# A transformer block on one core: a steady tile's scores wait for the values alone, and the orders of four engines are written anew

## The chip, the cores and the metric

The kernel runs on one core of a Trainium2 chip. The metric is the device time of one execution in microseconds (us), the median of three runs.

## What is computed

For 128 sequences of 64 tokens with 256 channels, everything in float32:

```python
n1 = g1(cond) * x / rms(x) + b1(cond)
x1 = x + softmax(q k^T / 4) v @ Wo.T              # 16 heads of 16
n2 = g2(cond) * x1 / rms(x1) + b2(cond)
out = x + x1 + (silu(n2 @ gate.T) * (n2 @ hid.T)) @ out.T   # hidden width 1024
```

g1, b1, g2 and b2 are small linear maps of a 64-wide condition of each sequence.

## The kernel before

**Tiles.** 16 tiles of 8 sequences (512 tokens). Products are made of float32 values split in a high part and a low rest (three passes: high by high, high by low, low by high), so most matrices exist as `_hi` and `_lo`. In PSUM eight banks are shared out by hand.

**Pipeline.** Tile t does its attention while the MLP of tile u = t - 1 runs between its pieces. Five instruction streams are written by hand: TensorE (PE), ScalarE (ACT), VectorE (DVE), GpSimd (POOL), SyncE (SP, all transfers). Each stream has functions for single pieces and four lists that call them: `first_tile` (t = 0, attention alone), `steady_tile` (t = 1 to 14; 2 to 14 in a loop), `last_tile` (t = 15) and `after_last` (the MLP of tile 15). Each engine works its list strictly in order, and each piece begins with semaphore waits. What decides the time is therefore which piece stands behind which on the same engine.

**Pieces on PE.** `gate(u, j)` and `hid(u, j)` are six matmuls of 512 columns each (lines 1221 to 1240), for chunk j of the hidden width. `down(u, j)` is twelve of 256 columns (lines 1082 to 1084). `scores(t, r)` (line 1183) is 64 small ones for half r of the heads, `transpose_probs(t, p)` (line 1193) four transposes, `values_probs(t, r)` (line 1208) 64 small ones. `project_q`, `project_k` (lines 1110 to 1113, six matmuls of 512 columns) and `project_v` (twelve of 256 columns) make the next tile's queries, keys and values, `project_out` (24 of 256 columns) closes this tile's attention, and `transpose_norm2(t, c)` (line 1102) turns the normed rows.

**Gate path.** gate(u, j), then tanh (ACT, line 506), silu (DVE, line 836), hidden (DVE, line 843, which needs hid too), high_hidden (ACT, line 511), low_hidden (POOL, line 284), then down(u, j). gate(u, j + 1) waits for silu(u, j), since the gate has one bank; hid(u, j + 1) waits for hidden(u, j).

**Softmax path.** scores, row_maxima and shift (DVE, lines 806, 813), exp (ACT, line 516), reciprocals (DVE, lines 820, 825), divide (POOL, line 290), transpose_probs, keep_transposed (ACT, line 521), values_probs, high_attention (ACT, line 526), low_attention (DVE, line 830), project_out.

**Norm paths.** Next tile: squares1 (ACT), next_inverse (POOL), two transfers that spread the factors, scale_rows (DVE, line 737), first_norm1 (DVE, lines 756 and 763) and second_norm1 (ACT, line 451), high_norm1 (ACT), low_norm1 (POOL), projections. This tile, behind project_out: first_residual (DVE, line 894), squares2 (ACT, line 442), inverse2 (POOL, lines 264, 267), scale_second (ACT, line 553) with scale_second_rest (DVE, line 746), transpose_norm2, second_norm2 (ACT, line 451) and first_norm2 (DVE), high_norm2 (ACT, line 477), low_norm2 (POOL line 278, DVE line 777). The last piece of ACT's list is `first_values(t + 1)` (line 500), which copies half the next tile's values from PSUM; DVE's is `second_values` (line 800).

**Start of a tile.** `scores(t, 0)` is PE's first piece. In a steady tile it waits for seven counts, one after the other:

```python
pe.wait_ge(k_act_done, t + 1)
pe.wait_ge(k_dve_done, t + 1)
pe.wait_ge(q_act_done, t + 1)
pe.wait_ge(q_dve_done, t + 1)
pe.wait_ge(v_act_done, t + 1)
pe.wait_ge(v_dve_done, t + 1)
pe.wait_ge(x1_done, 2 * t)
```

**SP.** In its order, each with its wait: the transposed input of the next tile, the store of a finished tile (waits for results), the next input x (waits for keep_input and squares1), then the factors out and back in (waits for next_inverse). In the first tile the output weights' transfer stands ahead of these.

Of the kernel before, what the change touches and what calls it, by code (L numbers as in the profile page):

```python
# [53 lines left out]
def conditioned_block(nc, x, xT, condT, modT, attW, gateT, hidT, outT, consts, out):  # L54
# [3 lines left out]
    with ExitStack() as ctx:  # L58
# [196 lines left out]
        def _(pool):  # L255
# [92 lines left out]
            def steady_tile(t, finish, ahead):  # L348
                u = t - 1
                sum_of_inputs(u)  # L350
                low_hidden(u, 0)
                divide(t, 0)
                divide(t, 1)
                low_hidden(u, 1)
                divide(t, 2)
                next_inverse(t)
                divide(t, 3)
                low_hidden(u, 2)
                low_hidden(u, 3)
                divide(t, 4)  # L360
                low_hidden(u, 4)
# [5 lines left out]
                low_hidden(u, 5)  # L367
                low_hidden(u, 6)
                inverse2(t)
# [3 lines left out]
            def last_tile(t, finish, ahead):  # L373
                u = t - 1
                divide(t, 0)
                low_hidden(u, 0)
                divide(t, 1)
                divide(t, 2)
                low_hidden(u, 1)
                divide(t, 3)  # L380
                low_hidden(u, 2)
                sum_of_inputs(u)
                divide(t, 4)
                low_hidden(u, 3)
                divide(t, 5)
                low_hidden(u, 4)
                divide(t, 6)
                divide(t, 7)
                low_hidden(u, 5)
# [32 lines left out]
        def _(act):  # L422
# [139 lines left out]
            def first_tile(t, ahead):  # L562
                u = t - 1
                high_hid_weights()
                keep_input(t)
                first_values(0)
                exp(t, 0)
                exp(t, 1)
                squares1(t + 1)
                exp(t, 2)  # L570
                exp(t, 3)
                exp(t, 4)
                keep_transposed(t, 0)
                keep_transposed(t, 1)
                high_out_weights()
                exp(t, 5)
                exp(t, 6)
                keep_transposed(t, 2)
                keep_transposed(t, 3)
                high_attention(t, 0)  # L580
                exp(t, 7)
                keep_transposed(t, 4)
                keep_transposed(t, 5)
                second_norm1(t + 1)
                high_norm1(t + 1, 0)
                high_norm1(t + 1, 1)
                keep_transposed(t, 6)
                keep_transposed(t, 7)
                high_attention(t, 1)
# [9 lines left out]
            def steady_tile(t, finish, ahead):  # L599
# [3 lines left out]
                high_hidden(u, 0)  # L603
# [3 lines left out]
                exp(t, 2)  # L607
                high_hidden(u, 1)
                tanh(u, 2)
                exp(t, 3)  # L610
                squares1(t + 1)
                tanh(u, 3)
                keep_transposed(t, 0)
                keep_transposed(t, 1)
                high_hidden(u, 2)
                tanh(u, 4)
                keep_transposed(t, 2)
                keep_transposed(t, 3)
                high_hidden(u, 3)
                high_attention(t, 0)  # L620
                exp(t, 4)
                exp(t, 5)
                tanh(u, 5)
                high_hidden(u, 4)
# [4 lines left out]
                exp(t, 6)  # L629
                exp(t, 7)  # L630
                high_hidden(u, 5)
                tanh(u, 6)
# [3 lines left out]
                high_hidden(u, 6)  # L636
                tanh(u, 7)
                first_queries(t + 1)
                high_attention(t, 1)
                first_keys(t + 1)  # L640
                squares2(t)
                scale_second(t)
                high_hidden(u, 7)
# [5 lines left out]
            def last_tile(t, finish, ahead):  # L649
# [3 lines left out]
                tanh(u, 1)  # L653
                high_hidden(u, 0)
                exp(t, 1)
                exp(t, 2)
                tanh(u, 2)
                high_hidden(u, 1)
# [823 lines left out]
```

## Time and profile before

| | us |
|---|---|
| median of three runs | 959.45 (959.16 to 959.62) |
| the profiled execution's own time | 959.58 |
| its span (first to last profiled instruction) | 957.5 |
| PE busy in the span | 908.0 |
| DVE, ACT, POOL busy | 664.8, 559.4, 451.9 |
| tile 1 to tile 15, start of scores to start of scores | 79.64 to 870.88 |
| last instruction of PE | 953.18 |

How to read it: the first 80 us are weights and tile 0, then 14 steady tiles repeat, then come tile 15 and the MLP that is left. An engine's busy time is the union of its instructions; a matmul's end is modelled and overlaps the start of the next by 0.16 us here, so the spacing of starts is the better measure. Times named as "at 41.8" below are counted from the start of scores(t, 0) of a tile.

### The profile page before, as it was taken

What the parts mean: (1) busy time and instruction counts of PE and PEld (TensorE: products, weight loads), DVE (VectorE), ACT (ScalarE), POOL (GpSimd) and SP (SyncE); (2) the same over time, 40 slices, a digit from 0 to 9 for tenths busy, and PEclk for the clock granted to TensorE, in tenths of its full rate; (3) what the DMA queues carried; (4) which work ended last, traced back from release to release, by engine and by line L of the source; (5) the groups of instructions that cost most, each with busy time, mean ns of one, the idle gap of its engine ahead of it and who ended that gap; (6) DMA issues with size and microseconds to landing.
All of it is one profiled execution on the core that took longest, in us unless ns stands there. A gap on an engine that the chain in (4) does not pass through costs nothing.

```text
span 957.5 us, 24194 instructions
## 1 busy us (share of the span) xinstructions
PE 908.0 (95%) x8988; PEld 773.5 (81%) x8988; DVE 664.8 (69%) x1082; ACT 559.4 (58%) x1255; POOL 451.9 (47%) x394
## 2 busy tenths in 40 slices
PE   5678999999999999999999999999999999999998
PEld 4466888878888887888888888888888888788887
DVE  3647768576875857778586877858687685868652
ACT  4556656656665666656566655655666566565542
POOL 4454525354463545436354543535455354544433
PEclk9779999999999999999999999999999999999999
DMA  5300101010110101011010111101010010200000
GB/s 191 98 26 23 34 25 56 1 55 22 44 33 22 39 16 55 22 44 33 7 47 22 44 32 44 33 0 55 22 44 33 23 53 0 55 0 1 24 23 23
DMA packets 25595, 34.06 MB, mean 36 GB/s; under 512 B 3296, under 2 KB 20896, under 8 KB 25440
## 3 DMA queue, kind: packets, MB, share of 16 engines
q1 hardware_dynamic: 25344, 33.59, 11.2%
q8 instruction: 18, 0.29, 0.1%
q10 hardware_dynamic: 224, 0.10, 0.0%
q14 instruction: 9, 0.07, 0.0%
HBM read 25.27 MB, written 8.42 MB: 35 GB/s over the span
## 4 chain that ended last, share of the span: by engine, by line
PE 82%; ACT 6%; issue 5%; DVE 3%; POOL 2%; DMA 1%; ACTq 1%; DVEq 0%; SPq 0%; POOLq 0%
PE ps L1082 8%; PE ps L1084 7%; PE ps L1083 7%; PE ps L1221 7%; PE ps L1237 6%; PE ps L1193 6%; PE ps L1227 6%; PE ps L1222 6%; PE ps L1240 6%; PE ps L1238 6%; PE ps L1183 4%; PE ps L1110 4%; PE ps L1208 4%; PE ps L1111 3%; PE ps L1113 3%
## 5 line engine op out<-in xcount | busy, mean ns | idle before, releaser
L284 POOL TENSOR_TENSOR h_lo<-h,h_hi 128x512 fp32r<-128x512 f32 x128 | 165.7, 1295 | 142.4 <-ACT h_hi L511 142.4
L290 POOL TENSOR_TENSOR probs<-probs,recip 128x512 f32<-128x512 f32 x128 | 134.5, 1058 | 105.6 <-DVE recip L825 105.5
L1082 PE MATMUL ps<-out_w_hi,h_hi 128*128 128x256 f32 x512 | 147.2, 287 | 0.7
L1084 PE MATMUL ps<-out_w_hi,h_lo 128*128 128x256 f32 x512 | 144.4, 282 | 0.0
L1083 PE MATMUL ps<-out_w_lo,h_hi 128*128 128x256 f32 x512 | 144.1, 281 | 0.0
L506 ACT ACTIVATE shared<-ps 128x512 f32<-128x512 f32 x128 | 76.1, 595 | 99.7 <-PE ps L1227 99.4
L836 DVE SCALAR_TENSOR_TENSOR shared<-shared,ps 128x512 f32<-128x512 f32 x128 | 87.4, 683 | 46.4 <-ACT shared L506 44.9
L516 ACT ACTIVATE probs<-probs 128x512 f32<-128x512 f32 x128 | 80.7, 631 | 62.5 <-DVE probs L813 61.9
L1221 PE MATMUL ps<-xn_hi,gate_w_hi 128*128 128x512 f32 x256 | 110.2, 430 | 0.4 <-DVE shared L836 0.2
L843 DVE SCALAR_TENSOR_TENSOR h<-shared,ps 128x512 f32<-128x512 f32 x128 | 87.4, 683 | 30.1 <-PE ps L1240 28.7
L1237 PE MATMUL ps<-xn_hi,hid_w_hi 128*128 128x512 f32 x256 | 105.1, 410 | 0.0
L1082 PEld LDWEIGHTS ps<-out_w_hi,h_hi 128*128 128x128 f32 x512 | 96.5, 188 | 8.2 <-POOL h_lo L284 6.5
L1222 PE MATMUL ps<-xn_hi,gate_w_lo 128*128 128x512 f32 x256 | 101.1, 395 | 0.0
L1238 PE MATMUL ps<-xn_hi,hid_w_lo 128*128 128x512 f32 x256 | 100.5, 393 | 0.0
L1083 PEld LDWEIGHTS ps<-out_w_lo,h_hi 128*128 128x128 f32 x512 | 96.4, 188 | 1.5
L1084 PEld LDWEIGHTS ps<-out_w_hi,h_lo 128*128 128x128 f32 x512 | 96.4, 188 | 0.0
L806 DVE TENSOR_REDUCE row_max<-ps 128x8 f32<-128x512 f32 x128 | 83.7, 683 | 17.5 <-PE ps L1183 17.2
L511 ACT CAST h_hi<-h 128x512 fp32r<-128x512 f32 x128 | 79.5, 622 | 25.6 <-DVE h L843 25.1
L820 DVE TENSOR_REDUCE sums<-probs 128x8 f32<-128x512 f32 x128 | 86.3, 674 | 3.4 <-ACT probs L516 1.9
L813 DVE TENSOR_TENSOR probs<-ps,row_max 128x512 f32<-128x512 f32 x128 | 87.3, 684 | 1.6 <-PE ps L1193 1.6
L1193 PE MATMUL ps<-consts_sb,probs 128*128 128x128 f32 x512 | 74.2, 282 | 8.2 <-POOL probs L290 8.1
L521 ACT COPY probsT<-ps 128x512 f32<-128x512 f32 x128 | 70.9, 587 | 17.4 <-PE ps L1193 17.4
(92 smaller groups left out, 2016.6 us busy)
## 6 DMA issues: line engine op xcount, KB each, us to landing
x_in<-in_x SPq DMA_DIRECT2D x16, 512.0 KB, 3.4
xT_in<-in_xT SPq DMA_DIRECT2D x16, 512.0 KB, 3.2
out<-result SPq DMA_DIRECT2D x15, 512.0 KB, 3.0
inv_all<-inv_rows SPq DMA_DIRECT2D x15, 256.0 KB, 3.8
shared<-in_attT SPq DMA_DIRECT2D x1, 1024.0 KB, 7.8
shared<-in_gateT SPq DMA_DIRECT2D x1, 1024.0 KB, 9.7
shared<-in_hidT SPq DMA_DIRECT2D x1, 1024.0 KB, 5.0
shared<-in_outT SPq DMA_DIRECT2D x1, 1024.0 KB, 5.7
```

Of the source, the lines that this page charges most:

```text
L284: nc.gpsimd.tensor_tensor(h_lo[:, j % KEPT, :], h[:, j % 2, :], h_hi[:, j % KEPT, :].bitcast(F32), ALU.subtract).then_inc(h_lo_done, 1)
L290: nc.gpsimd.tensor_tensor(own, own, recip[:, p % TOGETHER, :].unsqueeze(2).to_broadcast([P, SEQS, L]), ALU.mult).then_inc(divided, 1)
L836: nc.vector.scalar_tensor_tensor(act_g[:, :], act_g[:, :], 1.0, ps[:, GATE, :], ALU.add, ALU.mult).then_inc(silu_done, 1)
L843: nc.vector.scalar_tensor_tensor(h[:, j % 2, :], act_g[:, :], 0.5, ps[:, HIDDEN, :], ALU.mult, ALU.mult).then_inc(h_done, 1)
L1082: nc.tensor.matmul(dst, a_hi, b_hi, start=first, stop=False, skip_group_check=skip)
L1083: nc.tensor.matmul(dst, a_hi, b_lo, start=False, stop=False, skip_group_check=skip)
L1084: return nc.tensor.matmul(dst, a_lo, b_hi, start=False, stop=last, skip_group_check=skip)
L1193: last = nc.tensor.transpose(ps[:, bank_of(t, p), k * P:(k + 1) * P], probs[:, p % TOGETHER, k * P:(k + 1) * P], ident)
L1221: nc.tensor.matmul(ps[:, GATE, :], gate_w_hi[:, i, w], xn2_hi[:, i, :], start=i == 0, stop=False)
L1222: nc.tensor.matmul(ps[:, GATE, :], gate_w_lo[:, i, w], xn2_hi[:, i, :], start=False, stop=False)
L1237: nc.tensor.matmul(ps[:, HIDDEN, :], hid_w_hi[:, i, w], xn2_hi[:, i, :], start=i == 0, stop=False)
L1238: nc.tensor.matmul(ps[:, HIDDEN, :], hid_w_lo[:, i, w], xn2_hi[:, i, :], start=False, stop=False)
```

## The change

Two things. The first steady-tile wait is cut from seven counts to two:

```diff
                 elif r == 0:
-                    pe.wait_ge(k_act_done, t + 1)
-                    pe.wait_ge(k_dve_done, t + 1)
-                    pe.wait_ge(q_act_done, t + 1)
-                    pe.wait_ge(q_dve_done, t + 1)
+                    pe.wait_ge(v_dve_done, t + 1)
                     pe.wait_ge(v_act_done, t + 1)
-                    pe.wait_ge(v_dve_done, t + 1)
-                    pe.wait_ge(x1_done, 2 * t)
```

The lists of PE, ACT, DVE and POOL are written anew in all four functions; SP's is not touched, and every piece is called as often as before. Of `steady_tile`, in the order of the calls (T is transpose_probs, VP values_probs, KT keep_transposed, rm row_maxima, sh shift, rc reciprocals, low_h low_hidden):

```
PE before: scores0 gate0 hid0 gate1 hid1 down0 gate2 hid2 T0 gate3 T1 hid3 gate4 T2 T3 hid4
           scores1 VP0 gate5 down1 down2 hid5 down3 gate6 T4 T5 down4 hid6 q0 T6 T7 gate7 VP1
           q1 k0 project_out down5 hid7 k1 v1 tnorm0 tnorm1 v0 down6 down7
PE after:  scores0 gate0 hid0 gate1 hid1 T0 gate2 hid2 down0 gate3 hid3 T1 T2 gate4 T3 hid4
           scores1 VP0 down1 down2 gate5 down3 down4 hid5 T4 T5 gate6 hid6 q0 k0 T6 T7 gate7
           VP1 q1 hid7 project_out k1 v1 down5 tnorm0 tnorm1 v0 down6 down7

ACT before: tanh0 exp0 high0 keep_input tanh1 exp1 exp2 high1 tanh2 exp3 squares1 tanh3 KT0 KT1
            high2 tanh4 KT2 KT3 high3 high_attention0 exp4 exp5 tanh5 high4 second_norm1
            high_norm1(0,1) KT4 exp6 exp7 high5 tanh6 KT5 KT6 KT7 high6 tanh7 first_queries
            high_attention1 first_keys squares2 scale_second high7 second_norm2 high_norm2(0,1)
            first_values
ACT after:  tanh0 exp0 keep_input tanh1 exp1 high0 high1 tanh2 exp2 squares1 KT0 exp3 high2 tanh3
            KT1 tanh4 KT2 KT3 high_attention0 high3 exp4 exp5 high4 tanh5 second_norm1
            high_norm1(0,1) KT4 exp6 tanh6 exp7 KT5 KT6 KT7 first_keys tanh7 high_attention1
            high5 first_queries squares2 scale_second high6 high7 second_norm2 high_norm2(0,1)
            first_values

DVE before: low_norm2 results rm0 rm1 sh0 silu0 hidden0 rm2 rm3 rc0 sh1 silu1 sh2 hidden1 rc1 sh3
            silu2 rc2 hidden2 rc3 silu3 hidden3 silu4 hidden4 rm4 rm5 sh4 rm6 rc4
            low_attention0 sh5 scale_rows rc5 silu5 first_norm1 sh6 rm7 hidden5 sh7 rc6 rc7
            silu6 hidden6 low_attention1 second_queries first_residual silu7
            scale_second_rest hidden7 second_keys first_norm2 second_values
DVE after:  low_norm2 results rm0 rm1 sh0 silu0 hidden0 rc0 sh1 silu1 rm2 hidden1 sh2 rm3 rc1
            silu2 hidden2 sh3 rc2 rc3 silu3 hidden3 silu4 hidden4 rm4 rm5 sh4 sh5 scale_rows
            rc4 rc5 low_attention0 first_norm1 silu5 rm6 hidden5 sh6 rm7 sh7 rc6 rc7 silu6
            hidden6 low_attention1 silu7 second_queries first_residual hidden7 second_keys
            scale_second_rest first_norm2 second_values

POOL before: sum_of_inputs low_h0 divide0 divide1 low_h1 divide2 next_inverse divide3 low_h2
             low_h3 divide4 low_h4 divide5 low_norm1(0,1) divide6 divide7 low_h5 low_h6
             inverse2 low_h7 low_norm2
POOL after:  sum_of_inputs divide0 low_h0 low_h1 divide1 next_inverse divide2 divide3 low_h2
             low_h3 low_h4 divide4 divide5 low_norm1(0,1) divide6 divide7 low_h5 inverse2
             low_h6 low_h7 low_norm2
```

Of `first_tile`, what the prediction speaks of:

```diff
 ACT:
+                exp(t, 0)
                 high_hid_weights()
                 keep_input(t)
+                exp(t, 1)
+                exp(t, 2)
+                squares1(t + 1)
                 first_values(0)
-                exp(t, 0)
-                exp(t, 1)
-                squares1(t + 1)
-                exp(t, 2)
                 exp(t, 3)
...
 POOL:
-                low_hid_weights()
                 divide(t, 0)
                 divide(t, 1)
+                divide(t, 2)
                 next_inverse(t)
-                divide(t, 2)
                 divide(t, 3)
+                low_hid_weights()
                 divide(t, 4)
...
 PE:
                 scores(t, 0)
+                project_v(0, 1)
                 project_q(0, 1)
-                project_v(0, 1)
+                transpose_probs(t, 0)
                 project_v(0, 0)
                 scores(t, 1)
-                transpose_probs(t, 0)
                 transpose_probs(t, 1)
...
                 project_v(t + 1, 1)
+                project_v(t + 1, 0)
                 transpose_norm2(t, 0)
                 transpose_norm2(t, 1)
-                project_v(t + 1, 0)
```

`last_tile` is reordered along the same lines (transposes later among the gates, project_out followed by hid7, down3 and down4, then transpose_norm2; results(t - 2) moves to the front of DVE's list). In `after_last` four `down` pieces move by one place and results(t - 2) moves ahead of silu(u, 1).

## Rows read from the trace of the kernel before

**Rows 1.** Busy time by stretch: a steady tile, then tile 15 (stretch, length, engines, clock).
```profile
250.00:306.45 56.45, 55.52 (x561) 47.43 (x561) 41.19 (x67) 34.42 (x78) 26.99 (x24) 1.00 0.10 33
...
870.88:918.54 47.66, 46.70 (x513) 39.98 (x513) 33.02 (x59) 25.63 (x55) 22.86 (x20) 1.00 0.04 13
```

**Rows 2.** Timeline (start, length, instruction) at the end of the tile from 250.00.
```profile
300.28 1.04 PE L1102 MATMUL ps<-consts_sb,shared 128*128 128x128 f32 x8
...
304.92 1.19 ACT L500 COPY values<-ps 64x512 f32<-64x512 f32 x2
...
306.45 1.20 PE L1183 MATMUL ps<-keys,queries 32*64 32x128 f32 x64 [0.86 <-ACT values L500]
```

**Rows 3.** Timeline, the start of that tile: first instructions of PE's pieces, and silu(u, 0).
```profile
252.62 0.40 PE L1237 MATMUL ps<-xn_hi,hid_w_hi 128*128 128x512 f32 x1
...
254.19 0.50 PE L1221 MATMUL ps<-xn_hi,gate_w_hi 128*128 128x512 f32 x1
...
255.68 0.40 PE L1237 MATMUL ps<-xn_hi,hid_w_hi 128*128 128x512 f32 x1
...
257.31 0.39 PE L1082 MATMUL ps<-out_w_hi,h_hi 128*128 128x256 f32 x1
...
258.83 0.39 PE L1221 MATMUL ps<-xn_hi,gate_w_hi 128*128 128x512 f32 x1
...
260.23 0.39 PE L1237 MATMUL ps<-xn_hi,hid_w_hi 128*128 128x512 f32 x1
...
253.45 0.69 DVE L836 SCALAR_TENSOR_TENSOR shared<-shared,ps 128x512 f32<-128x512 f32 x1 [0.23 <-ACT shared L506]
```

**Rows 4.** Timeline of PE, the middle: T4 and T5, down4, hid6, q0, T6 and T7, gate7.
```profile
279.89 1.03 PE L1193 MATMUL ps<-consts_sb,probs 128*128 128x128 f32 x8
280.68 0.37 PE L1082 MATMUL ps<-out_w_hi,h_hi 128*128 128x256 f32 x1
...
282.31 0.50 PE L1237 MATMUL ps<-xn_hi,hid_w_hi 128*128 128x512 f32 x1
...
283.87 0.50 PE L1110 MATMUL ps<-xn_hi,att_w_hi 128*128 128x512 f32 x1
...
285.37 1.16 PE L1193 MATMUL ps<-consts_sb,probs 128*128 128x128 f32 x8
286.29 0.48 PE L1221 MATMUL ps<-xn_hi,gate_w_hi 128*128 128x512 f32 x1
```

**Rows 5.** Timeline: first matmuls of project_out and of down5 behind it, and scale_second.
```profile
291.78 0.28 PE L1082 MATMUL ps<-att_w_hi,attT_hi 128*128 128x256 f32 x1
...
294.62 0.28 PE L1082 MATMUL ps<-out_w_hi,h_hi 128*128 128x256 f32 x1
...
297.92 0.91 ACT L553 ACTIVATE shared<-shared,inv 128x256 f32<-128x256 f32 x2 [1.46 <-POOL inv L267]
```

**Rows 6.** Timeline behind scores(t, 1): rm4 and rm5, high_attention0; and the sums of rc6.
```profile
270.29 1.29 DVE L806 TENSOR_REDUCE row_max<-ps 128x8 f32<-128x512 f32 x2 [0.39 <-PE ps L1183]
...
271.35 0.59 ACT L526 CAST attT_hi<-ps 128x512 fp32r<-128x512 f32 x1 [2.38 <-PE ps L1208]
...
282.77 0.68 DVE L820 TENSOR_REDUCE sums<-probs 128x8 f32<-128x512 f32 x1
```

**Rows 7.** Timeline of DVE and POOL: scale_rows and divide7 of tile 0, divide5 and first_norm1.
```profile
53.02 1.97 DVE L737 TENSOR_TENSOR xn<-xT_in,inv_all 128x1024 f32<-128x1024 f32 x1
53.18 2.72 POOL L290 TENSOR_TENSOR probs<-probs,recip 128x512 f32<-128x512 f32 x1 [1.88 <-DVE recip L825]
...
278.03 1.04 POOL L290 TENSOR_TENSOR probs<-probs,recip 128x512 f32<-128x512 f32 x1
...
278.25 1.37 DVE L756 TENSOR_TENSOR xn<-xn,mod 128x512 f32<-128x512 f32 x1
279.76 0.69 DVE L763 TENSOR_TENSOR xn<-xn,mod 128x512 f32<-128x512 f32 x1
```

**Rows 8.** Timeline of tile 0: low_hid_weights, squares1, scores(0, 1).
```profile
28.13 4.60 POOL L297 TENSOR_TENSOR hid_w_lo<-shared,hid_w_hi 128x2048 fp32r<-128x2048 f32 x1 [2.40 <-ACT hid_w_hi L433]
...
35.46 0.42 ACT L442 ACTIVATE squares<-x_in 128x256 f32<-128x256 f32 x1 [0.45 <-DMA x_in<-in_x]
35.52 1.97 PE L1183 MATMUL ps<-keys,queries 32*64 32x128 f32 x64 [2.89 <-DVE queries L791]
```

More of the change, by code:

```diff
@@ L367, in steady_tile @@
                 low_hidden(u, 5)
+                inverse2(t)
                 low_hidden(u, 6)
-                inverse2(t)
                 low_hidden(u, 7)
@@ L606, in steady_tile @@
                 exp(t, 1)
-                exp(t, 2)
+                high_hidden(u, 0)
                 high_hidden(u, 1)
                 tanh(u, 2)
+                exp(t, 2)
+                squares1(t + 1)
+                keep_transposed(t, 0)
                 exp(t, 3)
-                squares1(t + 1)
+                high_hidden(u, 2)
                 tanh(u, 3)
-                keep_transposed(t, 0)
                 keep_transposed(t, 1)
-                high_hidden(u, 2)
                 tanh(u, 4)
@@ L679, in last_tile @@
                 tanh(u, 6)
-                keep_input(t)
                 high_attention(t, 1)
-                high_hidden(u, 5)
+                tanh(u, 7)
                 high_hidden(u, 6)
                 squares2(t)
-                tanh(u, 7)
                 scale_second(t)
@@ L966, in steady_tile @@
                 shift(t, 4)
[L967 to L969 removed]
                 shift(t, 5)
                 scale_rows(t + 1)
+                reciprocals(t, 4)
                 reciprocals(t, 5)
+                low_attention(t, 0)
+                first_norm1(t + 1)
                 silu(u, 5)
[L974 removed]
+                row_maxima(t, 6)
+                hidden(u, 5)
                 shift(t, 6)
                 row_maxima(t, 7)
[L977 removed]
                 shift(t, 7)
@@ L995, in last_tile @@
                 low_norm2(u)
+                results(t - 2)
                 row_maxima(t, 0)
@@ L998, in last_tile @@
                 shift(t, 0)
+                silu(u, 0)
                 shift(t, 1)
-                silu(u, 0)
-                row_maxima(t, 2)
                 hidden(u, 0)
                 reciprocals(t, 0)
+                silu(u, 1)
+                reciprocals(t, 1)
+                hidden(u, 1)
+                row_maxima(t, 2)
                 row_maxima(t, 3)
-                silu(u, 1)
+                silu(u, 2)
                 shift(t, 2)
-                hidden(u, 1)
-                reciprocals(t, 1)
+                hidden(u, 2)
+                shift(t, 3)
                 reciprocals(t, 2)
-                silu(u, 2)
-                shift(t, 3)
-                hidden(u, 2)
+                silu(u, 3)
                 reciprocals(t, 3)
-                silu(u, 3)
-                results(t - 2)
                 hidden(u, 3)
                 silu(u, 4)
+                hidden(u, 4)
                 row_maxima(t, 4)
@@ L1020, in last_tile @@
                 shift(t, 4)
+                shift(t, 5)
+                low_attention(t, 0)
                 row_maxima(t, 6)
-                hidden(u, 4)
-                shift(t, 5)
                 reciprocals(t, 4)
-                reciprocals(t, 5)
                 row_maxima(t, 7)
@@ L1036, in last_tile @@
                 hidden(u, 6)
+                silu(u, 7)
                 first_residual(t)
-                silu(u, 7)
                 hidden(u, 7)
@@ L1396, in last_tile @@
                 values_probs(t, 1)
+                gate(u, 7)
+                project_out(t, ahead)
+                hid(u, 7)
                 down(u, 3)
-                project_out(t, ahead)
-                gate(u, 7)
-                hid(u, 7)
                 down(u, 4)
```

164 lines of the change are left out of this document (80 added, 84 removed).

## Prediction

> **What bounds the kernel now.** I read the engines' busy times first: TensorE is busy 55.5 of 56.45 us in a steady tile, at full granted clock, and no other engine over 42 [rows 1]. The fourteen steady tiles repeat this to 0.02 us (the first is 1 us longer), so one of them, from 250.00, is read piece by piece. TensorE's own work is left as it is; what a new order can give is its idle time, which is seen in the spacing of starts, not in the modelled ends. An undisturbed gate or hid piece takes 1.40 us (258.83 to 260.23) [rows 3]. Three places are longer.
>
> 1. The end: scores(t, 0) starts with 0.86 us of idle time before it, released by first_values on ScalarE [rows 2]; the same line recurs at the start of 15 tiles. The values end at 304.92 + 1.19 = 306.11 and the scores start at 306.45, so 0.34 us pass between a release and its use. Between silu(u, 0), which ends at 254.14, and gate(u, 1), at 254.19, only 0.05 us pass [rows 3].
> 2. The start: hid(u, 0) takes 1.57 (waiting for silu) and gate(u, 1) 1.49, since a piece that follows a stall loses a further 0.1. hid(u, 1) takes 1.63 because down0 waits for the low part on GpSimd, and down0 then 1.52 against 1.42 [rows 3].
> 3. The middle: down4 takes 1.63 where 1.42 and 0.09 for coming behind transposes are due, hid6 1.56, q0 1.50, and T6 with T7 0.92 where T4 with T5 take 0.79 [rows 4]: 0.12 + 0.16 + 0.10 + 0.13 = 0.51 us.
>
> **The change in a steady tile, step by step.** Times "at" count from the start of scores(t, 0).
>
> Start. gate1 still waits for silu0 (the path gate, tanh, silu is not shortened): 0.26 us stay. down0 moves behind hid2, three pieces later, and T0 comes into its place. divide0 is now first behind the input sum on GpSimd and would be ready at 7.0, T0 is wanted at 7.1. So (1.63 - 1.40) + (1.52 - 1.42) = 0.33 goes. Gain 0.33.
>
> Middle. down1 to down4 and hid5 come ahead of T4, and q0 with k0 ahead of T6, so low parts, divides and low_norm1 all get 1 to 2 us more. The 0.51 us go, if the other engines are not later than now. Gain 0.51.
>
> What could make them later is scale_rows, now directly behind sh5. In the trace divide7 of tile 0 starts 0.16 us after a scale_rows and takes 2.72 instead of 1.04 us, to 0.9 us after its end; and first_norm1's first half, started 0.22 us after a divide, takes 1.37 instead of 0.69 [rows 7]. So of two such instructions the later one is held. In the new order: row maxima 4 and 5 and two shifts stand ahead of scale_rows, each 0.60 us after the other [rows 6], so it comes 2.40 us after rm4. high_attention0 starts 1.06 us after rm4 (271.35 - 270.29), then come its 0.5, high3's 0.6 and a handover of 0.1: low_h3 starts 2.25 us after rm4, first by 0.15 us. So scale_rows is held: 1.3 - 0.15 - 0.15 = about 1.0 us. Later first_norm1 meets divide5 as it does now, 0.7 us. Without holding silu5 would end 2.4 + 2.0 + 2 x 0.9 (two reciprocals [rows 6]) + 0.6 + 1.25 + 0.7 = 8.7 us after rm4; gate6 is wanted at 0.9 + 0.1 + 2.84 + 1.40 + 2.84 + 1.40 + 0.79 = 10.3 after rm4. The slack is 1.55 and the holds are 1.65 to 1.7: loss 0.1 us. (If VectorE came first, low_h3 would be held to 4.4 + 1.2 = 5.6 after rm4 where down3 wants it at 5.3: loss 0.3 and 0.1 for the stall, so 0.3 more than I take.)
>
> The Trainium skill has this as a rule ("SBUF — State Buffer", section "Who interferes with whom"): a VectorE instruction with two SBUF inputs and a GpSimd instruction that reads SBUF exclude each other, and whoever issues first blocks the other fully. It speaks against packing scale_rows beside low_h3 and low_h4. The trace agrees: 2.72 against 1.04 us [rows 7].
>
> Tail. project_out starts at 41.78 now (291.78 - 250.00) [rows 5]. New: 41.78 - 0.33 - 0.51 + 1.40 (hid7 now ahead of it) + 0.10 = 42.44. Behind it now come down5, hid7, k1, v1, and transpose_norm2 starts 8.50 after project_out (300.28 - 291.78) [rows 2, 5], though scale_second was ready at 7.05 (298.83 - 291.78). New: project_out 2.84 (294.62 - 291.78), k1 1.40, v1 1.42, down5 1.42: 7.08, a dead heat with the 7.05 + 0.05 of the chain residual, squares2, inverse2, scale_second. I take 7.10. From transpose_norm2 to the end of first_values it is 5.83 us (306.11 - 300.28) [rows 2], the same ScalarE pieces as before; high6 and high7 fit in the gap ahead of second_norm2. TensorE itself needs 0.8 + 1.5 + 1.4 + 1.5 = 5.2, so ScalarE still sets the start of the next tile.
>
> The wait. The removed counts are met long before; what they cost is that two more waits stand behind v_act_done. With v_act_done last, the handover should shrink from 0.34 towards the 0.05 of silu to gate [rows 2, 3]. Bounds: 0 (the start of 64 small matmuls is what costs) and 0.29. I take 0.29, since the handover with one wait is the nearest row.
>
> Period: 42.44 + 7.10 + 5.83 + 0.05 = 55.42 against 56.45, so 1.03 us a tile, and 14 tiles give 14.4 us.
>
> **Tile 0.** exp0 now precedes the hid weights' cast and keep_input on ScalarE, so SP's transfer of x is issued near 33.8 (29.0 now), and squares1, which waits for that transfer now already [rows 8], stands ahead of first_values: about 3.4 us of landing and 1.7 of squares put scores(0, 1) near 40 instead of 35.5. Against that, T0 runs early, and shift4, which waits for T0, is 1.3 us late instead of 4.5. low_hid_weights (4.60 us on GpSimd [rows 8]) goes from an idle stretch to a place before divide4, and divides 6 and 7 then meet scale_rows, each held in turn. Before transpose_norm2 v0 now stands, where TensorE sat idle. Bounds 0 (all absorbed by TensorE's idle stretches) and +4.6 (scores' delay in full); taken +1.6.
>
> **Tile 15 and after.** Tile 15 spans 47.66 with TensorE busy 46.70 [rows 1]; results ahead of the maxima lets silu0 come in time (0.2), down0 is put behind, and transpose_norm2 meets its chain. Bounds 0 and -1.5, taken -1.0. In after_last the stalls gate, tanh, silu, gate stay three in number: 0.
>
> **Sum.** 959.58 (the profiled execution, 2.1 above its span and 0.13 above the median) - 14.4 + 1.6 - 1.0 = 945.8. Median and profiled execution agree so well that no shift is made.
>
> **Rivals.** A difference of 0.2% (1.9 us) is about what a measurement of this kernel can tell from none.
> - A, forecast: 945.8, between 941 (no holds, tile 0 free) and 950. For it: stall by stall the trace shows what goes. Chance 0.52.
> - B, the handover stays 0.34: 14 x 0.29 = 4.1 more, 949.9. For it: the scores have a load of weights per small matmul. Against it: silu to gate. 0.12.
> - C, VectorE is first in the pair, or T0 or transpose_norm2 loses its dead heat each time: 0.3 a tile more, 950. 0.12.
> - D, only the wait counts; the new order loses in the middle what it gains: 14 x 0.29 = 4.1 and tile 0's loss: 959.6 - 4.1 + 1.6 - 1.0 = 956.1. 0.10.
> - E, slower: one more hold. If add_shift or scale_rows meets a second GpSimd piece (low_h4 follows low_h3 by one exp and one cast), 1.1 us falls straight on gate6, since the slack of 1.55 is spent. The period is then 56.5, and 14 x 0.07 + 0.6 = 1.6 us are lost: 961.2. It decides from holds of 2.6 us a tile (1.55 of slack and 1.03 of gain) on. Against it: the reciprocals lie between the pairs. 0.08. (By the rule of the Trainium skill above, the one that issues later is blocked fully, so such a further hold would cost its whole length.)
> - F, gains and losses of D and E mix to nothing: 0.03. G, better than 941 because DVE's list has slack I counted as spent: 0.03.
>
> **How the numbers follow.** Faster: A, B, C, D, G = 0.89; same 0.03, with a piece of D and E 0.04; slower 0.07. The range 941 to 956 leaves out E, F, G and part of D.
>
> **What would show it.** In the changed profile: starts of scores 55.4 us apart; the idle time before scores 0.6 to 0.7, first_values to scores 0.05; down0 at 1.42 and no stall around T6; scale_rows 2.9 us long beside low_h3; project_out at 42.4 and transpose_norm2 7.1 behind it; scores(0, 1) near 40. Wrong would be: scale_rows at 2.0 (then the period is 55.3), an idle line before gate6 of over 0.3, or scores 0.3 us behind first_values still.

## The result and the profile after

| | before | after |
|---|---|---|
| median of the comparison's 4 runs, us | 959.54 (959.16 to 961.56) | 949.56 (947.61 to 950.45) |
| ratio to before | | 0.9886 [0.9867, 0.9905] |
| span of the profiled execution | 957.5 | 947.4 |

The change makes the kernel 10.0 us faster; 13.7 were forecast. The range held the time, and the direction and most of the mechanism were right. TensorE still makes up most of the chain that ended last (87%, 82% before); GpSimd's busy time has grown from 451.9 to 488.0 us, though it does the same work. From the page of the kernel after (engines, costliest groups):

```profile
PE 900.7 (95%) x8988; PEld 772.5 (82%) x8988; DVE 675.1 (71%) x1082; ACT 552.1 (58%) x1255; POOL 488.0 (52%) x394
...
L284 POOL TENSOR_TENSOR h_lo<-h,h_hi 128x512 fp32r<-128x512 f32 x128 | 192.0, 1505 | 206.4 <-ACT h_hi L511 204.9
```

Where the 10 us come from is read in windows from one start of scores(t, 0) to the next, which is what [rows 1] show of the kernel before. Columns: length, then busy time (count) of PE, PE's loads, DVE, ACT and POOL, then granted clock, DMA share, GB/s. Tile 0, tile 1, tile 4 and tile 15 of the kernel after:

```profile
26.70:81.88 55.18, 34.00 (x400) 28.11 (x399) 33.74 (x54) 29.73 (x66) 25.98 (x18) 0.70 0.16 53
81.88:139.23 57.35, 56.82 (x560) 48.92 (x561) 40.73 (x66) 33.71 (x78) 29.54 (x24) 0.96 0.08 25
250.27:305.81 55.54, 54.84 (x560) 47.28 (x561) 41.82 (x68) 33.93 (x78) 29.50 (x24) 1.00 0.11 33
861.13:908.40 47.27, 46.60 (x512) 39.93 (x513) 33.61 (x60) 25.63 (x55) 23.01 (x20) 1.00 0.04 13
```

In the kernel before tile 0 (from 26.96) took 52.68, tile 1 57.45. So, by spans:

| stretch | before | after | difference | forecast |
|---|---|---|---|---|
| up to the first scores | 26.96 | 26.70 | -0.26 | 0 |
| tile 0 | 52.68 | 55.18 | +2.50 | +1.6 |
| tile 1 | 57.45 | 57.35 | -0.10 | -1.03 |
| tiles 2 to 14, each | 56.44 | 55.53 | -0.91, 13 times: -11.9 | -1.03, 13 times: -13.4 |
| tile 15 | 47.66 | 47.27 | -0.39 | -1.0 |
| MLP of tile 15, end | 38.96 | 39.00 | +0.04 | 0 |

These spans fall short of the forecast by 3.7 us, which lie in four places: 0.9 in tile 0, 0.9 in tile 1, 1.5 in the loop, 0.6 in tile 15 (against them, 0.3 ahead of the first scores, a stretch that takes 25.75 to 27.45 in the profiles of this study although no edit touches it).

**The end of a steady tile.** The timeline of the kernel after from 348 to 362 (start, length, engine, line, operation; in brackets the idle time before it and what ended it). This tile starts at 305.81, so project_out stands at 42.40 and transpose_norm2 7.10 behind it:

```profile
348.21 0.28 PE L1082 MATMUL ps<-att_w_hi,attT_hi 128*128 128x256 f32 x1
...
354.34 0.91 ACT L553 ACTIVATE shared<-shared,inv 128x256 f32<-128x256 f32 x2 [1.46 <-POOL inv L267]
...
355.31 1.09 PE L1102 MATMUL ps<-consts_sb,shared 128*128 128x128 f32 x8
...
360.00 1.19 ACT L500 COPY values<-ps 64x512 f32<-64x512 f32 x2
...
361.33 0.93 PE L1180 MATMUL ps<-keys,queries 32*64 32x128 f32 x45 [0.66 <-ACT values L500]
```

The values end at 360.00 + 1.19 = 361.19 and the scores start at 361.33: the handover, 0.34 in [rows 2], is 0.14 now, not the 0.05 that was forecast. transpose_norm2 has no idle line and yet starts 0.06 behind the end of scale_second (355.25): the dead heat that was forecast.

**The middle.** The other engines in the same tile, where the forecast had two holds (one of two instructions waits for the other inside its own run), and then the first matmul of project_k(t + 1, 0):

```profile
328.07 1.30 POOL L284 TENSOR_TENSOR h_lo<-h,h_hi 128x512 fp32r<-128x512 f32 x1 [5.66 <-ACT h_hi L511]
328.23 2.99 DVE L737 TENSOR_TENSOR xn<-xT_in,inv_all 128x1024 f32<-128x1024 f32 x1
...
329.63 2.76 POOL L284 TENSOR_TENSOR h_lo<-h,h_hi 128x512 fp32r<-128x512 f32 x1 [0.26 <-ACT h_hi L511]
...
332.35 2.56 POOL L290 TENSOR_TENSOR probs<-probs,recip 128x512 f32<-128x512 f32 x2
...
333.33 0.68 DVE L756 TENSOR_TENSOR xn<-xn,mod 128x512 f32<-128x512 f32 x1
...
334.15 1.31 DVE L763 TENSOR_TENSOR xn<-xn,mod 128x512 f32<-128x512 f32 x1
...
335.38 0.67 DVE L836 SCALAR_TENSOR_TENSOR shared<-shared,ps 128x512 f32<-128x512 f32 x1
...
339.75 0.57 ACT L521 COPY probsT<-ps 128x512 f32<-128x512 f32 x1
...
340.46 0.47 PE L1110 MATMUL ps<-xn_hi,att_w_hi 128*128 128x512 f32 x1
```

low_hidden(u, 3) starts first, by 0.16 us, and scale_rows takes 2.99 instead of 1.97. Then the hold is handed on: low_hidden(u, 4), started while scale_rows is still running, takes 2.76 for 1.29. first_norm1 is held in its second half (1.31 for 0.68) and not in its first. silu(u, 5) ends at 335.38 + 0.67 = 336.05 and gate(u, 6) runs at 336.14, directly behind T5, with no gap: with a handover of 0.05, 0.04 us of its slack are left. project_q and project_k(t + 1, 0) together take 2.94 (from 339.00 to 341.94) where two undisturbed pieces take 2.80: project_k waits for keep_transposed(t, 5), which ends at 340.32, and starts at 340.46. This stall of 0.14 was not forecast.

**Tile 0 and tile 15** of the kernel after, where the forecast took +1.6 and -1.0:

```profile
37.03 0.42 ACT L442 ACTIVATE squares<-x_in 128x256 f32<-128x256 f32 x1 [2.50 <-DMA x_in<-in_x]
...
38.64 1.16 ACT L500 COPY values<-ps 64x512 f32<-64x512 f32 x2
...
40.05 2.02 PE L1180 MATMUL ps<-keys,queries 32*64 32x128 f32 x64 [3.54 <-ACT values L500]
...
47.75 4.53 POOL L297 TENSOR_TENSOR hid_w_lo<-shared,hid_w_hi 128x2048 fp32r<-128x2048 f32 x1
...
52.24 6.27 POOL L290 TENSOR_TENSOR probs<-probs,recip 128x512 f32<-128x512 f32 x4
...
901.41 1.29 POOL L284 TENSOR_TENSOR h_lo<-h,h_hi 128x512 fp32r<-128x512 f32 x1
901.48 1.65 DVE L746 TENSOR_SCALAR shared<-shared,inv 128x256 f32<-128x256 f32 x2 [0.97 <-POOL inv L267]
...
903.22 0.96 PE L1102 MATMUL ps<-consts_sb,shared 128*128 128x128 f32 x7 [0.61 <-issue]
```

squares1 waits 2.50 us for x with first_values behind it, and scores(0, 1) start at 40.05 (35.52 in [rows 8]). low_hid_weights keeps divide(0, 4) until 52.24. In tile 15 scale_second_rest starts 0.07 us behind low_hidden(u, 6) and takes 1.65 us; transpose_norm2 follows it. The last line's "issue" names no cause: that TensorE waited for scale_second_rest is read from the order of the starts, and tried in the last experiment.

### The profile page after: what moved, and what is told of

It is laid out like the page before. It is cut to its first block, busy times and chain, and to the rows that moved or that the text cites. A ratio compares the mean times of both kernels' runs of the same rounds, so it can differ in the third digit from the quotient of the medians.

```text
span 947.4 us, 24151 instructions
## 1 busy us (share of the span) xinstructions
PE 900.7 (95%) x8988; PEld 772.5 (82%) x8988; DVE 675.1 (71%) x1082; ACT 552.1 (58%) x1255; POOL 488.0 (52%) x394
## 4 chain that ended last, share of the span: by engine, by line
PE 87%; ACT 6%; issue 2%; DVE 2%; DMA 1%; POOL 1%; ACTq 1%; SPq 0%; DVEq 0%
PE ps L1082 8%; PE ps L1084 7%; PE ps L1083 7%; PE ps L1218 7%; PE ps L1224 6%; PE ps L1234 6%; PE ps L1219 6%; PE ps L1237 6%; PE ps L1235 6%; PE ps L1190 6%; PE ps L1180 4%; PE ps L1110 4%; PE ps L1205 3%; PE ps L1111 3%; PE ps L1113 3%; ACT shared L451 3%
## 5 line engine op out<-in xcount | busy, mean ns | idle before, releaser
L284 POOL TENSOR_TENSOR h_lo<-h,h_hi 128x512 fp32r<-128x512 f32 x128 | 192.0, 1505 | 206.4 <-ACT h_hi L511 204.9
L290 POOL TENSOR_TENSOR probs<-probs,recip 128x512 f32<-128x512 f32 x128 | 141.1, 1117 | 69.2 <-DVE recip L825 68.8
L1234 PE MATMUL ps<-xn_hi,hid_w_hi 128*128 128x512 f32 x256 | 102.6, 401 | 0.0
L511 ACT CAST h_hi<-h 128x512 fp32r<-128x512 f32 x128 | 77.0, 613 | 16.2 <-DVE h L843 16.2
```

The lines of the kernel that those rows point to most:

```text
L284: nc.gpsimd.tensor_tensor(h_lo[:, j % KEPT, :], h[:, j % 2, :], h_hi[:, j % KEPT, :].bitcast(F32), ALU.subtract).then_inc(h_lo_done, 1)
L290: nc.gpsimd.tensor_tensor(own, own, recip[:, p % TOGETHER, :].unsqueeze(2).to_broadcast([P, SEQS, L]), ALU.mult).then_inc(divided, 1)
L1234: nc.tensor.matmul(ps[:, HIDDEN, :], hid_w_hi[:, i, w], xn2_hi[:, i, :], start=i == 0, stop=False)
```

## The experiments

The experiments were run in three groups, in which the kernel before took 960.86 (1 to 4), 959.76 (5 to 8) and 959.93 us (9 to 12). Differences of under 2 us between groups are therefore read from the traces and not from the medians. "Period" is the mean length of tiles 2 to 14.

**1 and 2. The wait alone, and the order alone.** The two waits in the kernel before, and the seven in the kernel after:

```diff
 # 1: before.  2: the same block, reversed, in after
                 elif r == 0:
-                    pe.wait_ge(k_act_done, t + 1)
...
-                    pe.wait_ge(x1_done, 2 * t)
+                    pe.wait_ge(v_dve_done, t + 1)
+                    pe.wait_ge(v_act_done, t + 1)
```

> The kernel before with the two counts of the change in place of the seven, all orders as before. Theory W (each wait that stands behind the last release costs about 0.1 us at the handover, and one is left): first_values to scores 0.15 us instead of 0.34, period 56.26 instead of 56.44, in all 14 to 15 x 0.19 = 2.8 us faster. Rival W0 (the handover is the start of 64 small matmuls): period 56.44, no change. Rival W1 (my prediction's figure): 0.05 us of handover, period 56.15, 4.1 us faster.

> The changed kernel with its seven counts back. Theory W: handover 0.34 again, period 55.53 + 0.19 = 55.72, 2.7 us slower than the changed kernel. Rival W0: 55.53. If the gain of the new order rested on the cut waits (another rival), the period would go up by more than 0.3.

Measured: with the wait alone 956.63 us, ratio 0.995 [0.9934, 0.9967], period 56.23; with the order alone 952.16 us, 0.991 [0.9894, 0.9927], period 55.74. A steady tile's end in the first:

```profile
249.80 1.20 ACT L500 COPY values<-ps 64x512 f32<-64x512 f32 x2
...
251.14 1.11 PE L1178 MATMUL ps<-keys,queries 32*64 32x128 f32 x59 [0.65 <-ACT values L500]
```

and in the second:

```profile
248.89 1.19 ACT L500 COPY values<-ps 64x512 f32<-64x512 f32 x2
...
250.43 1.20 PE L1183 MATMUL ps<-keys,queries 32*64 32x128 f32 x64 [0.85 <-ACT values L500]
```

251.14 - 251.00 = 0.14, and 250.43 - 250.08 = 0.35: the handover goes with the waits, whichever order stands around it. Both ways the waits are worth 0.21 us a tile (56.44 - 56.23, 55.74 - 55.53), so the two parts add up: of the 0.91 the wait brings 0.21 and the order 0.70. Rival D (only the wait counts) falls. In total, 1 is 4.2 us faster than before, which would fit rival W1's 4.1; its handover (0.14, not 0.05) and its period speak against W1, and 14 tiles by 0.21 are 2.9 us only. Where the rest came from is not shown: in the one profiled run tile 0 and tile 1 were longer than before, not shorter.

**3. The kernel after with the first tile's four lists of before.**

```diff
 def first_tile(t):      # PE, ACT, DVE, POOL
-    (the four lists of after)
+    (the four lists of before)
```

> The changed kernel with the four lists of tile 0 as before. Theory C (tile 0's new order costs 2.5 us in tile 0 itself and its longer idle stretches leave the clock low into tile 1): scores to scores 52.7 in tile 0 and 56.5 in tile 1 (57.35 with the new tile 0), 3.1 us faster than the changed kernel, about 946.5. Rival C0 (tile 1's first period is as long as it is for another reason): tile 1 stays at 57.35, 2.3 us faster.

Measured: 945.96 us (945.26 to 947.83), 0.985 [0.9834, 0.9867]. Tile 0 takes 53.70, and tile 1:

```profile
79.74:135.13 55.39, 54.84 (x561) 47.38 (x561) 40.76 (x66) 33.69 (x78) 29.64 (x24) 1.00 0.08 26
```

The median is 3.6 us below after: tile 0 is shorter by 1.5 and tile 1, whose lists are the same in both, by 2.0. The difference in tile 1 is in the third last column, the granted clock: 1.00 against 0.96. The total met the expectation (3.1), but neither part did: tile 0 was put at 52.7 and tile 1 at 56.5, and the two misses cancel.

The gain in tile 1 can't be put down to the old lists. Kernels before and 1 have these same lists in tile 0 and took 57.45 and 58.23 in tile 1, 1.0 and 2.0 us above their steady tiles. Here are the first scores of tile 1 in 1 and then in 3, after the same idle time:

```profile
80.39 2.02 PE L1178 MATMUL ps<-keys,queries 32*64 32x128 f32 x64 [3.29 <-ACT values L500]
```

```profile
79.74 1.20 PE L1180 MATMUL ps<-keys,queries 32*64 32x128 f32 x64 [3.29 <-ACT values L500]
```

So after 3.29 us without work the granted clock had fallen in one profile (0.50 in the 2 us from these scores on) and not in the other (1.00). With the new lists the idle time is 4.73 to 4.94 us, and in all eight profiles that have it (after, 2, and 4 to 9) tile 1 is 1.6 to 1.9 us longer than a steady tile. Tile 0 varies in the same way: with the old lists it took 52.68, 53.87 and 53.70 (before, 1, 3), with the new ones 55.10 to 55.18 in five profiles. So the new lists make tile 0 of the kernel after longer by 1.3 to 2.5 us, depending on the profile of the old ones that it is compared with.

**4. low_hid_weights at another place of the first tile.**

```diff
 # GpSimd, first_tile
     next_inverse(t)
-    divide(t, 3)
     low_hid_weights()
+    divide(t, 3)
     divide(t, 4)
```

> The changed kernel with low_hid_weights one place up in tile 0, between next_inverse and divide3, where GpSimd sits idle for 6.6 us. Theory L (divides 4 to 7 behind the 4.5 us of low_hid_weights collide with scale_rows): divide4 starts near 48 instead of 52.2, scale_rows and first_norm1 lose less holding, tile 0 is 0.8 us shorter. Rival L0 (tile 0's second half hangs on exp5, which waits for the fourth transpose): 0 to 0.2 us shorter.

Measured: 948.86 us, 0.9878 [0.9862, 0.9895]. divide(0, 4) comes at 47.05 instead of 52.24, yet tile 0 is only 0.44 us shorter (54.74), between theory L (0.8) and rival L0 (0 to 0.2): the second attention half then waits for keep_transposed, which stands behind second_norm1 on ScalarE. The forecast blamed this piece in part; it is a small part.

**5. A new end of the steady tile.** In the kernel after ScalarE's chain from project_out sets the next tile's start, so project_out goes one piece earlier, and down(u, 5) behind transpose_norm2, where TensorE was idle. project_out's wait for VectorE's queries is needed only from its third block on.

```diff
 # TensorE, steady_tile
     project_q(t + 1, 1)
-    hid(u, 7)
     project_out(t, ahead)
+    hid(u, 7)
     project_k(t + 1, 1)
     project_v(t + 1, 1)
-    down(u, 5)
     transpose_norm2(t, 0)
     transpose_norm2(t, 1)
+    down(u, 5)
 # project_out
-    if ahead: pe.wait_ge(q_dve_done, t + 2)
     for k in range(BLK):
+        if ahead and k == 2: pe.wait_ge(q_dve_done, t + 2)
 # VectorE: second_queries ahead of silu 7, scale_second_rest ahead of second_keys
```

> The changed kernel with a steady tile's end laid out anew: project_out waits for the queries' copy only ahead of its second half, and starts where hid7 stood; hid7, k1, v1, transpose_norm2, then down5, v0, down6, down7; DVE takes second_queries ahead of silu7 and scale_second_rest ahead of second_keys. Theory S (ScalarE's 5.9 us from transpose_norm2 on set the start of the next tile, and TensorE idles 0.6 us for it): project_out at 41.0 instead of 42.4, transpose_norm2 at 48.1 instead of 49.5, and 6.6 us of TensorE work behind it cover the chain: period 54.8 instead of 55.53, 14 x 0.73 = 10 us faster than the changed kernel, and no wait of scores for the values. Rival S0 (project_out cannot start earlier, the copies of the queries hold it): period 55.5 or above. Rival S1 (the residual chain is late for the earlier transposes): a stall before transpose_norm2 takes the place of the one before scores, period 55.2 or more.

Measured: 941.52 us (939.85 to 942.75), 0.9811 [0.979, 0.9831], 8.0 us better than after where 10 were expected; the period is 54.96 and not 54.8. A steady tile:

```profile
303.40:358.36 54.96, 54.93 (x561) 47.20 (x560) 41.35 (x67) 33.91 (x78) 29.52 (x24) 1.00 0.11 33
```

```profile
344.42 0.38 PE L1082 MATMUL ps<-att_w_hi,attT_hi 128*128 128x256 f32 x1
...
350.67 0.91 ACT L553 ACTIVATE shared<-shared,inv 128x256 f32<-128x256 f32 x2 [1.46 <-POOL inv L267]
351.63 1.09 PE L1102 MATMUL ps<-consts_sb,shared 128*128 128x128 f32 x8
```

project_out stands at 41.02 and transpose_norm2 at 48.23, 1.3 us earlier than in after (49.50). The 0.66 us of idle time before the scores are gone: TensorE is busy 54.93 of 54.96 us. So the end of the tile was bound by ScalarE's chain as argued, and a steady tile shows no idle time between its pieces any more. Short stalls inside them stay: project_out takes 2.95 us here (344.42 to 347.37) and 2.84 in after.

**6. silu(u, 5) one row maximum later** (tests the slack before gate(u, 6)).

```diff
 # VectorE, steady_tile
     first_norm1(t + 1)
-    silu(u, 5)
     row_maxima(t, 6)
+    silu(u, 5)
```

> The changed kernel with silu(u, 5) one place later, behind row_maxima(t, 6), 0.60 us. Theory M (the holds have eaten the whole slack of silu5 before gate6, as I reckoned): gate6 0.57 us later, period 56.1, 8 us slower than the changed kernel. Rival M0 (there is slack left there): period 55.53.

Measured: 955.96 us, 0.9962 [0.9948, 0.9976], 6.4 us slower than after, period 56.00, 0.47 more than after for an edit of 0.60 us. In a steady tile:

```profile
337.82 0.67 DVE L836 SCALAR_TENSOR_TENSOR shared<-shared,ps 128x512 f32<-128x512 f32 x1
...
338.54 0.51 PE L1218 MATMUL ps<-xn_hi,gate_w_hi 128*128 128x512 f32 x1 [0.32 <-DVE shared L836]
```

gate(u, 6) now waits for silu, released 0.05 us after its end, and starts at 30.89 in its tile instead of 30.33: 0.56 later, as theory M has it (0.57). The slack that the holds leave is therefore 0.04 us. The period loses less, 0.47, since project_q and project_k(t + 1, 0) take 2.79 here and not 2.94: the stall ahead of project_k in after is gone. So the slack before gate(u, 6) is spent, which was rival E's condition; rival E would have needed one more hold.

**7. scale_rows one reciprocal later** (takes it out of the way of low_hidden(u, 3)).

```diff
 # VectorE, steady_tile
     shift(t, 5)
-    scale_rows(t + 1)
     reciprocals(t, 4)
+    scale_rows(t + 1)
     reciprocals(t, 5)
```

> The changed kernel with scale_rows one place later, behind reciprocals(t, 4), so that it starts after low_h3 has ended. Theory P (a DVE instruction with two SBUF inputs is held by a GpSimd piece that started before it, here for 1.0 us): scale_rows takes 2.0 instead of 3.0 us, silu5 ends about 0.5 us earlier, and the period stays within 0.05 of 55.53 since TensorE has work until then. Rival P0 (scale_rows is long for another reason, its rows of factors): still 3.0 us, silu5 later, period 55.9 or more.

Measured: 951.90 us, 0.9915 [0.9898, 0.9932], period 55.79: slower than after by 0.26 a tile, where nearly nothing was expected.

```profile
328.94 1.30 POOL L284 TENSOR_TENSOR h_lo<-h,h_hi 128x512 fp32r<-128x512 f32 x1 [5.66 <-ACT h_hi L511]
...
330.44 2.00 DVE L737 TENSOR_TENSOR xn<-xT_in,inv_all 128x1024 f32<-128x1024 f32 x1
330.50 3.10 POOL L284 TENSOR_TENSOR h_lo<-h,h_hi 128x512 fp32r<-128x512 f32 x1 [0.25 <-ACT h_hi L511]
```

scale_rows is back at 2.00: its 2.99 was the hold. But it is now 0.06 us ahead of low_hidden(u, 4), which takes 3.10 us and ends 0.34 us later in the tile than in after, and down(u, 4) waits for it: down(u, 3) and down(u, 4) take 3.25 us together instead of 2.89. silu(u, 5) comes 0.27 later in its tile, where theory P had it 0.5 earlier, because both halves of first_norm1 are held now (1.40 and 1.31). That the hold is there is shown; the expectation's sum missed what stands behind it.

**8. first_values ahead of squares1 in the first tile** (on top of 4).

```diff
 # ScalarE, first_tile
     exp(t, 2)
-    squares1(t + 1)
     first_values(0)
+    squares1(t + 1)
```

> The kernel of the run before it in this study (low_hid_weights between next_inverse and divide3) with first_values ahead of squares1 on ScalarE in tile 0. Theory X (squares1 waits for the transfer of x, issued 4.5 us later than before, and holds first_values and with it scores(0, 1)): scores(0, 1) near 38.0 instead of 40.0, tile 0 2 us shorter than with the changed kernel. Rival X0 (tile 0 hangs on the factors' two transfers behind squares1, or on the softmax chain further on): scores(0, 1) 2 us earlier and tile 0 under 0.5 us shorter.

Measured: 946.67 us, 0.9867 [0.985, 0.9883]; tile 0 takes 52.38, 2.36 less than in 4.

```profile
36.23 1.17 ACT L500 COPY values<-ps 64x512 f32<-64x512 f32 x2 [1.47 <-PE ps L1084]
37.42 0.42 ACT L442 ACTIVATE squares<-x_in 128x256 f32<-128x256 f32 x1
37.77 1.20 PE L1180 MATMUL ps<-keys,queries 32*64 32x128 f32 x64 [1.59 <-DVE values L800]
```

Counted from scores(0, 0), scores(0, 1) start at 10.84 (13.21 in 4, 13.35 in after), and run in 1.20 us for 2.02 in after. Tile 0 is shorter by as much as they are earlier, which rules out rival X0. So the values, which did not need the transfer of x and stood behind the piece that did, held up tile 0 by 2.4 us, nearly all of its excess over before in the two profiles (2.50).

**9, 10 and 11. Both edits, and TensorE kept at work.** 9 is 5 with 8. 10 adds the kernel's own matmuls of weights, whose products are written to a bank that nobody reads, behind transpose_norm2 of tile 0; 11 adds such matmuls ahead of T3, T7 and the second attention half as well. What is computed stays the same.

```diff
 # TensorE, first_tile
     transpose_probs(t, 2)
+    pe.wait_ge(probsT_done, 1)      # 11
+    keep_clock_up(16, PAIR)         # 11
     transpose_probs(t, 3)
...
     transpose_probs(t, 6)
+    keep_clock_up(5, PAIR + 1)      # 11
     transpose_probs(t, 7)
+    keep_clock_up(7, PAIR + 1)      # 11
     values_probs(t, 1)
...
     transpose_norm2(t, 1)
+    keep_clock_up(16, Y + 1)        # 10 and 11
```

> The new end of a steady tile and both repairs of tile 0 (low_hid_weights between next_inverse and divide3, first_values ahead of squares1) on the changed kernel. Theory: the two sets of gains are in different stretches and add: 8.0 us of the tail and 2.9 us of tile 0, 949.6 - 10.9 = 938.7. Rival: tile 0's gain is lost in a late clock, 941.

> The run before with 16 matmuls on weights that nobody reads behind transpose_norm2 of tile 0, where TensorE sits idle for 4.7 us. Theory C (what tile 1 loses at its start is the granted clock at 1.2 GHz after that idle stretch): scores(1, 0) 1.2 us long instead of 2.0, gate0 1.7 instead of 2.6, tile 1 1.9 us shorter at 55.0. Rival C1 (the clock falls back anyway, or the fill runs at the low clock and makes scores late): no change or 1 to 2 us slower.

> The run before with such matmuls in three idle stretches more of tile 0 (16 ahead of the fourth transpose, 5 ahead of the eighth, 7 ahead of values_probs(0, 1)). Theory C: values_probs 1.1 us long instead of 1.9, transposes 0.6 instead of 1.1, q0 1.6 instead of 2.6, of which about 2 us lie on the chain of tile 0: 2 us faster. Rival C2 (tile 0 hangs on DVE and ScalarE there, not on the length of PE's pieces): under 0.5 us.

Measured: 9 takes 939.87 us, 0.9792 [0.9776, 0.9808], between its theory (938.7) and its rival (941), so the total does not decide; its tile 0 takes 52.61 and its period is 54.97, so both sets of gains are there. 10 takes 936.94 us, 0.9761 [0.9747, 0.9775]; 11 takes 935.34 us, 0.9745 [0.9731, 0.9758]. The start of tile 1 in 9, window and scores:

```profile
80.06:83.00 2.94, 2.94 (x66) 2.45 (x67) 1.01 (x3) 0.00 (x0) 2.39 (x1) 0.50 0.02 6
```

```profile
80.06 2.02 PE L1180 MATMUL ps<-keys,queries 32*64 32x128 f32 x64 [4.74 <-ACT values L500]
```

and in 10:

```profile
78.98:82.00 3.02, 3.02 (x72) 2.54 (x73) 1.97 (x4) 0.20 (x1) 2.41 (x1) 1.00 0.02 5
```

```profile
74.00 3.89 PE L1120 MATMUL ps<-att_w_hi 128*128 128x512 f32 x16
...
78.98 1.20 PE L1180 MATMUL ps<-keys,queries 32*64 32x128 f32 x64 [1.09 <-ACT values L500]
```

After 4.74 us without work TensorE is granted 0.50 (its 1.2 GHz level) and the same 64 matmuls take 2.02 us; after 1.09 us it is granted 1.00 and they take 1.20. Tile 1 falls from 56.84 to 54.94 us. That is the term the forecast did not have. (The rest of the 2.9 us between 9 and 10 is not in a stretch that the edit touches: the first scores start at 27.45 in 9 and at 26.44 in 10.) In 11 the second attention half of tile 0 runs in 1.14 us, where 10 takes 1.93 and 1.94 for its two:

```profile
59.49 1.14 PE L1205 MATMUL ps<-probsT,values 128*32 128x64 f32 x64 [0.27 <-ACT probsT L521]
```

and tile 0 falls by a further 1.7 us, to 50.84, where 2 were expected; rival C2 (under 0.5) falls.

**12. low_hidden(u, 6) ahead of inverse2 in the last tile** (on top of 11).

```diff
 # GpSimd, last_tile
     low_hidden(u, 5)
-    inverse2(t)
     low_hidden(u, 6)
+    inverse2(t)
```

> The run before with low_hidden(u, 6) ahead of inverse2 in the last tile on GpSimd. Theory P (scale_second_rest takes 1.6 us instead of 0.6 since low_hidden6 starts just before it, and transpose_norm2 waits 0.6 us for it): scale_second_rest 0.6 us long, transpose_norm2 0.7 us earlier, tile 15 46.6 instead of 47.3. Rival (low_hidden6 makes inverse2 late): no gain.

Measured: 934.67 us (933.84 to 934.92), 0.9737 [0.9724, 0.975]; tile 15 takes 46.54 (47.28 in 11, 47.27 in after).

```profile
887.76 0.62 DVE L746 TENSOR_SCALAR shared<-shared,inv 128x256 f32<-128x256 f32 x2 [0.96 <-POOL inv L267]
...
888.74 0.65 PE L1102 MATMUL ps<-consts_sb,shared 128*128 128x128 f32 x4
```

scale_second_rest takes 0.62, so its 1.65 in after was low_hidden(u, 6) beside it (in the kernel before it took 1.28), and transpose_norm2 comes 0.76 us earlier in its tile than in 11. The medians of 11 and 12 are only 0.7 us apart; it is the tile that shows the gain. Of all versions this is the fastest: 14.9 us below after (949.56) by medians, 14.3 by ratios, and by its ratio 2.6% below before.

## Why the prediction was right, and where it was not

- **Start and middle of the steady tile: right.** project_out was put at 42.44 and stands at 42.40, so the gains of 0.33 and 0.51 and the loss of 0.1 hold as a sum. There is no stall at down0, T6 or T7 in the trace. The loss lies elsewhere than forecast: gate(u, 6) kept 0.04 of slack and lost nothing, while project_k(t + 1, 0), one of the pieces that were said to get more time, lost 0.14 to keep_transposed(t, 5). That the two are of one size is luck.
- **The hold: right in size and in who is first.** low_hidden(u, 3) first by 0.15 was forecast, 0.16 is seen; scale_rows 2.9 against 2.99; silu(u, 5) left with next to no slack (0.04, experiment 6). Which half of first_norm1 is held was wrong, and that low_hidden(u, 4) is held too was not in the text; neither reached TensorE. Experiment 7 shows how near it stood: the hold moved by one instruction costs 0.26 a tile. The rule of the Trainium skill ("SBUF — State Buffer", "Who interferes with whom") that who issues first blocks the other holds in both directions here: in after GpSimd blocks scale_rows (1.97 to 2.99), in experiment 7 scale_rows blocks GpSimd (1.29 to 3.10).
- **Tail: right.** transpose_norm2 7.10 behind project_out (7.10 forecast), first_values' end 5.88 behind it (5.83), and ScalarE's chain still the bound, which experiment 5 shows by moving its start.
- **The handover: the term that was mis-sized.** "I take 0.29" from 0.34 - 0.05; it is 0.20 (0.34 to 0.14), the whole wait 0.21 a tile by period. The nearest row was taken to be silu to gate, but there the count that comes last is the last wait of its piece, and here it was not. With seven waits v_act_done stood two waits from the end, now it is the last, so two queued waits cost 0.20 together; that each costs 0.1 is a division, not a run of its own. Experiments 1 and 2 also take away and put back four waits ahead of v_act_done; that those cost nothing, because TensorE stands idle there for 0.65 us or more, is argued and not shown. What the last 0.09 is stays open: no run put a single wait there. It is 0.09 of the period's miss of 0.11, over 13 tiles 1.2 us of the 3.7.
- **Tile 0: the sign and the place right, the size not.** scores(0, 1) "near 40" are at 40.05, but only 1.6 of 4.6 us was taken to reach the end; between the two profiles 2.50 did. Against experiments 1 and 3, which have the old tile 0 too, it is 1.3 and 1.5, so the size is known to about 1 us only, and the 1.6 may have been nearer than the table says. "TensorE's idle stretches" absorb less than was said, and low_hid_weights, put among the causes, is worth 0.44 alone (experiment 4) while the order of first_values and squares1 is worth 2.36 (experiment 8).
- **Tile 1: a term that was missing.** 14 tiles by 1.03 counted tile 1 as a steady one. Tile 1 gained 0.10: it starts after a stretch in which TensorE has next to nothing to do, at half the clock. That the kernel before had a tile 1 "1 us longer" was seen and not asked about. Experiment 10, which keeps TensorE at work, gives back 1.9 us there, and experiment 3 had 2.0 less. Why the same tile 0 is followed by a full clock in experiment 3 and not in before or experiment 1 is open.
- **Tile 15: too large.** -1.0 taken, -0.39 found, which is what project_out moved (from 34.49 to 34.10 in the tile); from there to transpose_norm2 it is 7.99 us in both kernels. "transpose_norm2 meets its chain" failed: scale_second_rest was held for 1.0 us by low_hidden(u, 6), and experiment 12, which takes the hold away, brings tile 15 to 46.54, 1.1 below before. The Trainium skill (same section) names tensor_scalar among the VectorE instructions that can enter a two-port mode, when their operands meet its conditions, and then contend with GpSimd for the port pair that the two share. The trace agrees (0.62 against 1.65 us); the forecast applied the rule to instructions with two SBUF inputs alone.
- **The rivals.** B (handover stays) and C (dead heats lost) gave the measured 950 to within 0.5 us, and neither happened: the handover shrank, and the dead heats (pieces that were to be ready just in time) came out as forecast. A total that fits a rival proves nothing about it; the pieces decide. D falls by experiments 1 and 2, E and F by the measured gain, G by a time above 941.

## What to carry to other kernels

Price a repeated tile from its rows, and then price the first and the last tile as kernels of their own, with the clock that they leave to the next one: here two thirds of the shortfall (2.4 of 3.7 us) lay there. Where an engine other than TensorE sets the start of the next round, move the head of its chain earlier, and TensorE's free work behind it (8.0 us); then fill TensorE's idle stretches ahead of dense work (3.7 us in tiles 0 and 1). A wait that is long met still costs if it is queued behind the one that comes last, so put the last one last.

## What the runs showed of the hardware that was not expected

- After 4.74 us without work, the scores of tile 1 ran at a granted clock of 0.50 and took 2.02 us instead of 1.20 (experiments 9 and 10). After 3.29 us without work, they took 2.02 us in one profile (experiment 1) and 1.20 in another (experiment 3), with the same lists ahead of them. In the kernel after, the stretch before tile 1 has 0.27 us of TensorE's work in 5, and those that follow are granted 0.50, 0.60 and then 1.00 (windows, the granted clock is the third last column):

```profile
77.00:82.00 5.00, 0.27 (x10) 0.15 (x16) 3.80 (x5) 4.54 (x12) 1.75 (x2) 0.75 0.00 0
82.00:84.00 2.00, 2.00 (x65) 1.67 (x66) 0.08 (x2) 0.00 (x0) 2.00 (x1) 0.50 0.04 8
84.00:87.00 3.00, 3.00 (x9) 2.38 (x10) 1.87 (x3) 0.32 (x1) 0.27 (x1) 0.60 0.00 0
87.00:90.00 3.00, 2.98 (x13) 2.13 (x12) 2.51 (x5) 1.98 (x4) 0.26 (x1) 1.00 0.07 5
```

- A hold between VectorE and GpSimd is passed on: 2.99 on scale_rows, then 2.76 on low_hidden(u, 4); and again the two divides (2.56 for twice 1.04), then 1.31 on a half of first_norm1. That is most of why the mean of GpSimd's 128 low_hidden went from 1295 to 1505 ns, 27 us in all, with no work added: 14 times 1.47 us on low_hidden(u, 4) are 21.
- A VectorE instruction with one tensor input (scale_second_rest, 128x256 float32, two of them) is held as well: 1.65 us for 0.62.
